# Second layer's cross-attention: four max products in every pair of tiles, and the mask of even tiles copied for two PSUM banks at once

## The chip, the cores and the metric

One core of a Trainium2 chip runs the kernel. The metric is the device time in microseconds; lower is better. Below, TensorE is PE in the profile (PEld its weight loads), VectorE is DVE, ScalarE is ACT.

## The reference, cut to what matters

Two layers follow each other, each a cross-attention to a context of 4096 rows and two smaller blocks. The change touches the second layer's attention alone (batch 2, 256 query rows, 16 heads of 16):

```python
Q = query @ Wq.T + bq; K = key @ Wk.T + bk; V = value @ Wv.T + bv
energy = jnp.einsum('bhqd,bhkd->bhqk', Q, K) / np.sqrt(HEAD_DIM)
energy = jnp.where(mask == 0, jnp.float32(-1e+20), energy)
attention = jax.nn.softmax(energy, axis=-1)
x = jnp.einsum('bhqk,bhkd->bhqd', attention, V)
return x.transpose(0, 2, 1, 3).reshape(b, -1, D_MODEL) @ Wo.T + bo
```

## The kernel before, in words

**The steps.** An attention is cut into 8 steps: four groups of four heads times two batches. A step k handles four heads of one batch against all 4096 keys. It needs the largest score of every query row first, so two things run beside each other: the softmax of step k, and the row maxima of step k+1.

**A step's softmax** goes over 32 tiles of 128 keys. For a tile, TensorE writes the scores of four heads (keys on the partitions, 4 x 256 query rows) into two PSUM banks: banks 0 and 1 for an even tile, 2 and 3 for an odd one (`at_pe_scores`, L533, four matmuls of 256 columns). The row maximum is taken off in the same matmul: it stands, negated and split in three bf16 parts, in three extra rows of Q. ScalarE takes the exponential of both banks at once (`at_act_step`, L666, 128x1024), and TensorE multiplies with the values (`at_pe_values`, L546). In the second layer the mask is added in PSUM: the bank is first filled with the mask and the scores are accumulated onto it. Of each tile, the first bank is filled by TensorE (L525, identity times mask, 512 columns) and the second by ScalarE (L670, a copy of 128x512), right after it has read that bank's previous tile. Tiles 0 and 1 of a step have both banks filled by TensorE.

**Row maxima.** A step needs 64 max products, called units: TensorE computes scores of 128 query rows against 512 keys (`at_pe_unit`, L501), and VectorE adds the mask and reduces to a maximum (`at_dve_unit`, L587). They use the three banks 4, 5, 7 in turn, so TensorE can be three units ahead of VectorE (semaphore `at_seen`). After the 64th, VectorE works out the maximum and its three parts (`at_dve_top`, L622 to L630); TensorE transposes them with eight small matmuls (`at_pe_rows`, L512) into one of the three banks, and ScalarE copies them into Q (`at_act_rows`, L640). The third unit after these matmuls waits for ScalarE's copies (`at_qrows`).

**The order of the work** is written out. A step has 16 pairs of tiles, j = 0 to 15. `at_pe_step` issues, for pair j: some units, the scores of tile 2j+2, some units, the scores of tile 2j+3, some units, the values of tiles 2j and 2j+1. `UNITS_AT[j]` says how many units stand at the three places; the same table serves both layers. Units of pairs 0 to 12 belong to step k+1, those of pairs 13 to 15 (`OWN` = 13) already to step k+2. The row matmuls stand at the start of pair 14 (`ROWS_AT`). Pair 15 issues the scores of tiles 0 and 1 of the next step. `at_dve_step` follows the same table, with the maxima at the start of pair 13. `LEAD` units of step 1 are computed before step 0 (7), the first `DONE` of them (2) before the row matmuls (`at_pe`, `at_dve`). ScalarE's order is: exponential of tile i, then the mask of tile i+2; its row copies stand before the exponential of tile 30, the copy of the previous step's output after that of tile 1. In the last step there are no units, and ScalarE has a few extra activations in its middle.

**Loads.** SyncE loads keys and values in quarters, each when the values of the step before it have used its place (`at_load`).

Of the kernel before, what the change touches and what calls it, by code (L numbers as in the profile page):

```python
# [22 lines left out]
HG = 4  # L23
# [28 lines left out]
def units_at(k, j, part):  # L52

    first = sum(map(sum, UNITS_AT[OWN if j >= OWN else 0:j])) + sum(UNITS_AT[j][:part])
    first, k = (first, k + 2) if j >= OWN else (first + LEAD, k + 1)
    return [(k, first + m) for m in range(UNITS_AT[j][part] if k < STEPS else 0)]


def rows_before(k):

    return min(UNITS * (k + 1) + DONE, UNITS * STEPS)


def bank_turn(n):

    return n + max(0, n - DONE) // UNITS

# [9 lines left out]
def build(nc, A, out):  # L77
    ctx = ExitStack()
    with ctx:
# [398 lines left out]
        def unit_bank(k, u):  # L478
            return UBANK[bank_turn(UNITS * k + u) % 3]

        def rows_bank(k):
            return UBANK[(rows_before(k) + k) % 3]
# [5 lines left out]
        def at_pe_unit(e, L, k, u, bank=None):  # L488
# [6 lines left out]
            since = (n - DONE) % UNITS if n >= UNITS + DONE else UNITS  # L495
# [5 lines left out]
            e.matmul(PS[:, unit_bank(k, u) if bank is None else bank, :], Qz[0:ROWS, o:o + 128],  # L501
                     Kz[b][0:ROWS, hh, c * CH:c * CH + CH], start=True, stop=True).then_inc(sem("at_unit"), 1)

        def at_pe_rows(e, L, k):

            e.wait_ge(sem("at_mparts"), at_count(L, k, 1, 1))
            e.wait_ge(sem("at_seen"), at_count(L, 0, UNITS, rows_before(k) + 1))
            for hh in range(HG):
                p0 = 96 - 32 * (hh // 2)
                for tt in range(2):  # L510
                    o = (hh % 2) * T + tt * 128
                    m = e.matmul(PS[p0:p0 + 3, rows_bank(k), o:o + 128], mparts[:, :, 2 * hh + tt], identb[:, :],  # L512
                                 start=True, stop=True)
            m.then_inc(sem("at_rows"), 1)

        def at_pe_scores(e, L, k, i):
# [34 lines left out]
        def at_pe_units(e, L, k, j, part):  # L551
            for kk, u in units_at(k, j, part):
                at_pe_unit(e, L, kk, u)
# [16 lines left out]
        def at_dve_unit(e, L, k, u, bank=None):  # L570
            g, b = divmod(k, 2)
            q, hh, tt, c = unit(u)
            ps = PS[:, unit_bank(k, u) if bank is None else bank, :]
# [28 lines left out]
        def at_dve_units(e, L, k, j, part):  # L602
            for kk, u in units_at(k, j, part):
# [29 lines left out]
        def at_act_rows(e, L, k):  # L633
            g, b = divmod(k, 2)
            e.wait_ge(sem("at_rows"), at_count(L, k, 1, 1))
            for m_ in range(2):
# [3 lines left out]
                e.activation(to[:, :, b * T:b * T + T], PS[p0:p0 + 3, rows_bank(k), :].rearrange("p (h t) -> p h t", h=2),  # L640
# [10 lines left out]
        def at_act_step(e, L, k):  # L651
            for i in range(NT):
# [15 lines left out]
                if L == 1 and i + 2 < NT:  # L668
# [1086 lines left out]
```

## Time and profile before

| | us |
|---|---|
| median of 3 runs | 1411.46 |
| lowest, highest | 1409.7, 1416.26 |
| the profiled execution's own time | 1413.51 |
| its span | 1411.7 |

Over the span: TensorE busy 89%, VectorE 73%, ScalarE 66%, GpSimd 14%. "Busy" sums whole stages, and a matmul's end is modelled, so TensorE's share says little about whether it waits. The second layer's attention runs from about 883 to 1316 us of the span; before it 64 units of step 0 run alone, from 840.

### The profile page before, as it was taken

How to read it: one execution, taken by the hardware profiler on the slowest of the kernel's cores; microseconds unless marked ns; L12 is line 12 of the kernel's file. 1: busy time of each engine (PE TensorE's matmuls, PEld its weight loads, DVE VectorE, ACT ScalarE, POOL GpSimd, SP SyncE). 2: the span in 40 equal slices, each digit the busy share in tenths (PEclk: the TensorE clock that was granted, in tenths of full speed). 3: DMA queues.
4: the chain of work that ended last, by engine and by line, in shares of the span. 5: the costliest groups of instructions: out<-in, count | busy, mean ns of one | idle time of the engine just before them, and what ended most of it. 6: DMA issues, size and time to landing. Idle time of an engine off the chain costs nothing.

```text
span 1411.7 us, 25663 instructions
## 1 busy us (share of the span) xinstructions
PE 1253.6 (89%) x8952; PEld 649.6 (46%) x8952; DVE 1024.8 (73%) x2276; ACT 927.0 (66%) x1203; POOL 203.0 (14%) x183
## 2 busy tenths in 40 slices
PE   7759999999999999789998539999999999998745
PEld 3436544444444445345555311445444444443523
DVE  3318799999999951479998449778778778763256
ACT  2317757667766775267664190999999999999304
POOL 2212200000000000069995040000000000000000
PEclk9979989999999999999999755999999999999976
DMA  4998785455545310127776874144343443300000
GB/s 150 216 250 275 246 206 115 96 124 114 129 93 114 62 63 31 37 84 244 250 259 196 205 115 104 36 88 81 73 92 69 85 84 70 62 22 2 1 0 15
DMA packets 100683, 160.97 MB, mean 114 GB/s; under 512 B 8496, under 2 KB 57136, under 8 KB 100064
## 3 DMA queue, kind: packets, MB, share of 16 engines
q1 hardware_dynamic: 99088, 158.13, 45.4%
q10 hardware_dynamic: 1488, 1.42, 0.4%
q8 instruction: 67, 1.10, 0.3%
q14 instruction: 40, 0.33, 0.1%
HBM read 114.34 MB, written 45.18 MB: 113 GB/s over the span
## 4 chain that ended last, share of the span: by engine, by line
PE 64%; DVE 13%; issue 12%; ACT 6%; POOL 2%; DMA 1%; DVEq 1%; SPq 1%; POOLq 0%; ACTq 0%
PE PS L546 17%; PE PS L501 16%; PE PS L533 15%; PE PS L525 4%; PE PS L274 3%; ACT Pz L666 2%; PE PS L283 2%; DVE Vz L1031 2%; DVE OT L1039 2%; DVE Kz L1031 1%; DMA Pz<-in_ctxT 1%; ACT Pz L664 1%; PE PS L791 1%; PE PS L821 1%; PE PS L785 1%
## 5 line engine op out<-in xcount | busy, mean ns | idle before, releaser
L666 ACT ACTIVATE Pz<-PS 128x1024 f32<-128x1024 f32 x488 | 483.2, 1018 | 110.9 <-PE PS L533 108.4
L587 DVE CUSTOM_DVE_ANT_0 Pz<-PS,Tz 128x512 bf16<-128x512 f32 x512 | 334.4, 689 | 88.0 <-PE PS L501 83.2
L501 PE MATMUL PS<-Kz,Qz 96*128 96x512 bf16 x1024 | 365.9, 401 | 31.6 <-issue 21.2
L533 PE MATMUL PS<-Qz,Kz 99*128 99x256 bf16 x2048 | 313.1, 274 | 5.1 <-ACT Pz L664 3.0
L584 DVE TENSOR_REDUCE mx<-PS 128x1 f32<-128x512 f32 x448 | 289.6, 687 | 13.8 <-PE PS L501 13.2
L546 PE MATMUL PS<-Pz,Vz 128*17 128x256 f32 x4096 | 271.4, 383 | 0.2
L533 PEld LDWEIGHTS PS<-Qz,Kz 99*128 99x128 bf16 x2048 | 192.9, 98 | 129.5 <-ACT Pz L664 10.4
L501 PEld LDWEIGHTS PS<-Kz,Qz 96*128 96x128 bf16 x1024 | 99.4, 98 | 196.8 <-DVE mx L587 78.6
L546 PEld LDWEIGHTS PS<-Pz,Vz 128*17 128x17 f32 x4096 | 94.1, 97 | 132.0 <-issue 63.4
L670 ACT ACTIVATE PS<-Tz 128x512 f32<-128x512 bf16 x240 | 144.3, 601 | 7.6
L525 PE MATMUL PS<-Tz,identb 128*128 128x512 bf16 x272 | 104.8, 385 | 8.7 <-ACT Pz L666 8.5
L352 POOL TENSOR_TENSOR Pz<-Pz 128x512 bf16<-128x512 f32 x64 | 79.1, 1246 | 145.4 <-ACT Pz L314 145.2
L392 POOL TENSOR_TENSOR rstd<-vare,nhalf 128x4 f32<-128x4 f32 x6 | 6.1, 1013 | 590.7 <-DVE vare L381 590.7
L274 PE MATMUL PS<-Pz,Vz 128*128 128x512 f32 x128 | 64.0, 624 | 21.6 <-DMA Pz<-in_ctxT 15.2
L331 DVE TENSOR_TENSOR Pz<-PS,Pz 128x512 f32<-128x512 f32 x32 | 21.9, 688 | 58.3 <-ACT Pz L299 58.3
L283 PE MATMUL PS<-Kz,Pz 128*128 128x256 f32 x256 | 62.0, 385 | 2.5 <-ACT Pz L309 1.4
L299 ACT ACTIVATE Pz<-PS 128x512 bf16<-128x512 f32 x32 | 19.1, 597 | 67.0 <-DMA k_parts<-Pz 34.2
L937 ACT ACTIVATE PS<-Kz,acoef 128x510 f32<-128x510 f32 x64 | 42.8, 686 | 29.7 <-DVE Kz L1031 16.3
L283 PE MATMUL PS<-Vz,Pz 128*128 128x256 f32 x256 | 61.5, 383 | 0.7 <-ACT Pz L309 0.6
L274 PE MATMUL PS<-Pz,Kz 128*128 128x512 f32 x128 | 61.9, 606 | 0.0
L283 PEld LDWEIGHTS PS<-Kz,Pz 128*128 128x128 f32 x256 | 47.5, 190 | 28.3 <-ACT Pz L309 14.9
L581 DVE CUSTOM_DVE_ANT_0 Tz<-PS,Tz 128x512 bf16<-128x512 f32 x64 | 43.9, 686 | 19.3 <-PE PS L501 18.3
(218 smaller groups left out, 1211.1 us busy)
## 6 DMA issues: line engine op xcount, KB each, us to landing
k_parts<-Pz SPq DMA_DIRECT2D x192, 128.0 KB
Kz<-k_parts SPq DMA_DIRECT2D x64, 384.0 KB, 4.8
v_ones<-Pz SPq DMA_DIRECT2D x32, 544.0 KB, 4.9
Vz<-v_ones SPq DMA_DIRECT2D x64, 272.0 KB, 6.0
Pz<-in_ctxT SPq DMA_DIRECT2D x32, 512.0 KB, 5.8
Kz<-k_parts SPq DMA_DIRECT2D x64, 256.0 KB, 5.5
Kz<-k_parts SPq DMA_DIRECT2D x64, 128.0 KB, 5.9
Kz<-in_mask_pieces SPq DMA_DIRECT2D x16, 512.0 KB, 5.8
```

The source lines that it names most:

```text
L274: m = e.matmul(PS[:, 4 + half, :], wk[L][:, k, half * 128:half * 128 + 128], ctxb(s)[:, k, :], start=(k == 0), stop=(k == KC - 1))
L283: m = e.matmul(PS[:, 6, st * D:st * D + D], ctxb(s)[:, k, t * 128:t * 128 + 128], wv[L][:, k, :], start=(k == 0), stop=(k == KC - 1))
L352: e.tensor_tensor(kb(s, half, 2), kres(half), kb(s, half, 1), ALU.subtract)\
L501: e.matmul(PS[:, unit_bank(k, u) if bank is None else bank, :], Qz[0:ROWS, o:o + 128], Kz[b][0:ROWS, hh, c * CH:c * CH + CH], start=True, ...
L525: e.matmul(PS[:, bank, :].rearrange("p (h t) -> p h t", h=2), identb[:, :], maskTs[:, i:i + 1, :].broadcast_to([128, 2, T]), start=True, s ...
L533: m = e.matmul(PS[:, bank, o:o + T], Kz[b][0:KROWS, hh, i * 128:i * 128 + 128], Qz[0:KROWS, q:q + T], start=(L == 0), stop=True, skip_grou ...
L546: m = e.matmul(PS[32 * hh:32 * hh + VW, 6, 0:T], Vz[:, b, o:o + VW], probs(i)[:, hh * T:hh * T + T], start=(i == 0), stop=(i == NT - 1), s ...
L581: e.tensor_tensor_reduce(bjunk[:, u % 3, :], ps, bias_rows[:, hh, o:o + CH][:, ::-1], 1.0, LOWEST, ALU.add, ALU.max, to).then_inc(sem("at_ ...
L584: e.tensor_reduce(to, ps, AX.X, ALU.max).then_inc(sem("at_seen"), 1)
L587: e.tensor_tensor_reduce(junk[:, u % 3, :], ps, masks[:, tt, c * CH:c * CH + CH], 1.0, LOWEST, ALU.add, ALU.max, to).then_inc(sem("at_seen ...
L666: m = e.activation(probs(i), PS[:, 2 * (i % 2):2 * (i % 2) + 2, :].rearrange("p a n -> p (a n)"), ACT.Exp)
L670: e.activation(PS[:, 2 * (i % 2) + 1, :].rearrange("p (h t) -> p h t", h=2), maskTs[:, i + 2:i + 3, :].broadcast_to([128, 2, T]), ACT.Iden ...
```

## The change

It gives each layer a table of its own. The first layer's is the old one. The second layer's has (1, 1, 2) for every pair: four units in each of 16 pairs. So `LEAD` for the second layer is 12 (7 before) and `DONE` 4 (2 before). And the masks of the second layer: for even tiles from tile 2 on, ScalarE copies the mask into both banks with one activation of 128x1024, and TensorE adds none; for odd tiles, TensorE fills both banks and ScalarE copies nothing. TensorE's even scores wait for that copy ahead of the first of the four instead of the third.

```diff
-UNITS_AT = ((1, 1, 1),) + ((1, 2, 2), (1, 1, 2)) * 6 + ((1, 0, 1), (1, 1, 2), (0, 0, 1))
+UNITS_AT = (((1, 1, 1),) + ((1, 2, 2), (1, 1, 2)) * 6 + ((1, 0, 1), (1, 1, 2), (0, 0, 1)),
+            ((1, 1, 2),) * 16)
 OWN = 13
 ROWS_AT = 14
-LEAD = sum(map(sum, UNITS_AT[OWN:]))
-DONE = sum(map(sum, UNITS_AT[OWN:ROWS_AT]))
+def total(L, j0, j1):
+
+    return sum(map(sum, UNITS_AT[L][j0:j1]))
+
+
+LEAD = [total(L, OWN, NT // 2) for L in range(2)]
+DONE = [total(L, OWN, ROWS_AT) for L in range(2)]
...
+def units_at(L, k, j, part):
+
+    first = total(L, OWN if j >= OWN else 0, j) + sum(UNITS_AT[L][j][:part])
+    first, k = (first, k + 2) if j >= OWN else (first + LEAD[L], k + 1)
+    return [(k, first + m) for m in range(UNITS_AT[L][j][part] if k < STEPS else 0)]
...
 in at_pe_scores:
-                if L == 1 and (hh == 0 or hh == 2 and i < 2):
+                if L == 1 and hh % 2 == 0 and (i % 2 or i < 2):
                     e.matmul(PS[:, bank, :].rearrange("p (h t) -> p h t", h=2), identb[:, :],
                              maskTs[:, i:i + 1, :].broadcast_to([128, 2, T]), start=True, stop=False,
                              skip_group_check=True)
-                elif L == 1 and hh == 2:
-
-
-                    e.wait_ge(sem("at_masked"), at_count(0, k, NT - 2, i - 1))
+                elif L == 1 and hh == 0:
+
+
+                    e.wait_ge(sem("at_masked"), at_count(0, k, NT // 2 - 1, i // 2))
...
 in at_act_step:
-                if L == 1 and i + 2 < NT:
+                if L == 1 and i + 2 < NT and i % 2 == 0:
                     e.wait_ge(sem("at_exp"), at_count(L, k, NT, i + 3))
-                    e.activation(PS[:, 2 * (i % 2) + 1, :].rearrange("p (h t) -> p h t", h=2),
-                                 maskTs[:, i + 2:i + 3, :].broadcast_to([128, 2, T]), ACT.Identity)\
+                    e.activation(PS[:, 0:2, :].rearrange("p a (h t) -> p (a h) t", h=2),
+                                 maskTs[:, i + 2:i + 3, :].broadcast_to([128, HG, T]), ACT.Identity)\
                         .then_inc(sem("at_masked"), 1)
...
 in at_pe (at_dve alike):
-            for u in range(DONE):
+            for u in range(DONE[L]):
                 at_pe_unit(e, L, 1, u)
             at_pe_rows(e, L, 0)
             e.wait_ge(sem("at_ones"), B * HG * (L + 1))
-            for u in range(DONE, DONE + 2):
+            for u in range(DONE[L], DONE[L] + 2):
                 at_pe_unit(e, L, 1, u)
             for i in range(2):
                 at_pe_scores(e, L, 0, i)
-            for u in range(DONE + 2, LEAD):
+            for u in range(DONE[L] + 2, LEAD[L]):
                 at_pe_unit(e, L, 1, u)
```

The other lines pass the layer L on to `units_at`, `rows_before`, `bank_turn`, `unit_bank` and `rows_bank`, which read `DONE[L]` and `LEAD[L]`.

## Rows read from the trace of the kernel before

**Rows 1.** The page's first part: busy time and share of each engine
```profile
PE 1253.6 (89%) x8952; PEld 649.6 (46%) x8952; DVE 1024.8 (73%) x2276; ACT 927.0 (66%) x1203; POOL 203.0 (14%) x183
```

**Rows 2.** Busy us by stage: stage, length, PE, PEld, DVE, ACT, POOL, PEclk, DMA share, GB/s
```profile
830.00:886.00 56.00, 43.76 (x86) 8.81 (x87) 42.72 (x141) 19.21 (x9) 12.43 (x7) 0.50 0.64 115
1153.50:1207.00 53.50, 52.90 (x488) 26.41 (x487) 42.94 (x132) 50.03 (x65) 0.00 (x0) 1.00 0.43 81
1260.50:1316.00 55.50, 46.46 (x446) 18.75 (x447) 16.42 (x35) 54.14 (x73) 0.00 (x0) 1.00 0.05 15
```

**Rows 3.** The chain of waits, two pairs of a step: start, us, what
```profile
1111.77 0.32 PE PS L501
1112.09 0.22 PE PS L525
1112.31 0.44 PE PS L533 x4
...
1113.62 0.43 PE PS L501 x2
1114.06 0.99 PE PS L546 x16
...
1118.57 0.32 PE PS L501
```

**Rows 4.** Who waited for whom, 890 to 1310 us: total, times, longest
```profile
ACT Pz L666 <- PE PS L533: 16.6, 44, 0.8
```

**Rows 5.** The timeline at a seam between steps: start, us, engine, instruction, idle before
```profile
1151.79 0.39 PE L512 MATMUL PS<-identb,mparts 128*3 128x128 bf16 x8
...
1152.11 0.39 PE L501 MATMUL PS<-Kz,Qz 96*128 96x512 bf16 x1
...
1152.75 0.60 ACT L670 ACTIVATE PS<-Tz 128x512 f32<-128x512 bf16 x1
...
1154.61 1.94 ACT L666 ACTIVATE Pz<-PS 128x1024 f32<-128x1024 f32 x2
...
1154.64 0.61 PE L501 MATMUL PS<-Kz,Qz 96*128 96x512 bf16 x2 [0.60 <-ACT Qz L640]
```

**Rows 6.** The chain in the last step, two exponentials one pair apart
```profile
1279.40 1.02 ACT Pz L666
...
1282.55 1.02 ACT Pz L666
```

**Rows 7.** Groups by line and form, 890 to 1310 us
```profile
L666 ACT ACTIVATE Pz<-PS 128x1024 f32<-128x1024 f32 x250 | 252.5, 1013 | 18.4 <-PE PS L533 16.6
...
L670 ACT ACTIVATE PS<-Tz 128x512 f32<-128x512 bf16 x235 | 141.3, 601 | 7.5
```

**Rows 8.** The timeline before step 0
```profile
880.35 0.22 DVE L622 TENSOR_REDUCE mneg<-mx 128x8 f32<-128x64 f32 x1
...
881.38 0.69 DVE L587 CUSTOM_DVE_ANT_0 Pz<-PS,Tz 128x512 bf16<-128x512 f32 x1
...
883.36 0.61 PE L525 MATMUL PS<-Tz,identb 128*128 128x512 bf16 x1
...
886.75 1.97 PE L501 MATMUL PS<-Kz,Qz 96*128 96x512 bf16 x4
...
887.57 0.69 DVE L587 CUSTOM_DVE_ANT_0 Pz<-PS,Tz 128x512 bf16<-128x512 f32 x1 [3.25 <-PE PS L501]
...
888.18 0.69 DVE L587 CUSTOM_DVE_ANT_0 Pz<-PS,Tz 128x512 bf16<-128x512 f32 x1
888.32 0.10 PEld L501 LDWEIGHTS PS<-Kz,Qz 96*128 96x128 bf16 x1 [1.00 <-DVE mx L587]
...
888.55 0.38 PE L525 MATMUL PS<-Tz,identb 128*128 128x512 bf16 x1
```

**Rows 9.** The chain of waits, row copies at two seams in turn
```profile
1099.27 0.59 ACT Qz L640
...
1153.38 0.59 ACT Qz L640
```

More of the change, by code:

```diff
@@ L44, with rows_before, bank_turn @@
 STEPS = 2 * NG
-UNITS_AT = ((1, 1, 1),) + ((1, 2, 2), (1, 1, 2)) * 6 + ((1, 0, 1), (1, 1, 2), (0, 0, 1))
+UNITS_AT = (((1, 1, 1),) + ((1, 2, 2), (1, 1, 2)) * 6 + ((1, 0, 1), (1, 1, 2), (0, 0, 1)),
+            ((1, 1, 2),) * 16)
 OWN = 13
 ROWS_AT = 14
-LEAD = sum(map(sum, UNITS_AT[OWN:]))
-DONE = sum(map(sum, UNITS_AT[OWN:ROWS_AT]))
[L52 to L66, printed above, removed]
+def total(L, j0, j1):
[6 more added lines that the diff above has]
+    return [(k, first + m) for m in range(UNITS_AT[L][j][part] if k < STEPS else 0)]
+def rows_before(L, k):
+    return min(UNITS * (k + 1) + DONE[L], UNITS * STEPS)
+def bank_turn(L, n):
+    return n + max(0, n - DONE[L]) // UNITS
 def unit(u):
@@ L476, in at_load, with unit_bank, rows_bank @@
                 at_load_values(e, L, g, b, q)
[L478 to L482, printed above, removed]
+        def unit_bank(L, k, u):
+            return UBANK[bank_turn(L, UNITS * k + u) % 3]
+        def rows_bank(L, k):
+            return UBANK[(rows_before(L, k) + k) % 3]
         def at_count(L, k, scale, more=0):
@@ L494, in at_pe_unit @@
             n = UNITS * k + u
-            since = (n - DONE) % UNITS if n >= UNITS + DONE else UNITS
+            since = (n - DONE[L]) % UNITS if n >= UNITS + DONE[L] else UNITS
             if since == 2:
@@ L500, in at_pe_unit @@
             o = (HG * g + hh) * R + b * T + tt * 128
-            e.matmul(PS[:, unit_bank(k, u) if bank is None else bank, :], Qz[0:ROWS, o:o + 128],
+            e.matmul(PS[:, unit_bank(L, k, u) if bank is None else bank, :], Qz[0:ROWS, o:o + 128],
                      Kz[b][0:ROWS, hh, c * CH:c * CH + CH], start=True, stop=True).then_inc(sem("at_unit"), 1)
@@ L506, in at_pe_rows @@
             e.wait_ge(sem("at_mparts"), at_count(L, k, 1, 1))
-            e.wait_ge(sem("at_seen"), at_count(L, 0, UNITS, rows_before(k) + 1))
+            e.wait_ge(sem("at_seen"), at_count(L, 0, UNITS, rows_before(L, k) + 1))
             for hh in range(HG):
@@ L511, in at_pe_rows @@
                     o = (hh % 2) * T + tt * 128
-                    m = e.matmul(PS[p0:p0 + 3, rows_bank(k), o:o + 128], mparts[:, :, 2 * hh + tt], identb[:, :],
+                    m = e.matmul(PS[p0:p0 + 3, rows_bank(L, k), o:o + 128], mparts[:, :, 2 * hh + tt], identb[:, :],
                                  start=True, stop=True)
@@ L551, in at_pe_units @@
         def at_pe_units(e, L, k, j, part):
-            for kk, u in units_at(k, j, part):
+            for kk, u in units_at(L, k, j, part):
                 at_pe_unit(e, L, kk, u)
@@ L572, in at_dve_unit @@
             q, hh, tt, c = unit(u)
-            ps = PS[:, unit_bank(k, u) if bank is None else bank, :]
+            ps = PS[:, unit_bank(L, k, u) if bank is None else bank, :]
             if L == 0 and b == 0 and u == 0:
@@ L602, in at_dve_units @@
         def at_dve_units(e, L, k, j, part):
-            for kk, u in units_at(k, j, part):
+            for kk, u in units_at(L, k, j, part):
                 at_dve_unit(e, L, kk, u)
@@ L639, in at_act_rows @@
                 to = Qz[96:99, o:o + 2 * R].rearrange("p (h r) -> p h r", h=2)
[L640 removed]
+                e.activation(to[:, :, b * T:b * T + T], PS[p0:p0 + 3, rows_bank(L, k), :].rearrange("p (h t) -> p h t", h=2),
                              ACT.Identity).then_inc(sem("at_qrows"), 1)
@@ L731, in at_dve @@
             at_dve_top(e, L, 0)
-            for u in range(DONE + 2):
+            for u in range(DONE[L] + 2):
                 at_dve_unit(e, L, 1, u)
@@ L736, in at_dve @@
                     at_dve_bias(e, 0, i)
-            for u in range(DONE + 2, LEAD):
+            for u in range(DONE[L] + 2, LEAD[L]):
                 at_dve_unit(e, L, 1, u)
```

## The prediction, made before the changed kernel was run

> **What bounds the kernel now.** I read the page first. TensorE is busy for 89% of the span [rows 1], which hides stages with different limits, so I cut the span by stage. The change lies in the second layer's attention, from 883 to 1316 us. There the steps last about 54 us each. In one of them TensorE shows 52.90 us of work in 53.50, ScalarE 50.03 and VectorE 42.94, with the clock granted in full; in the last step, which has no max products, TensorE drops to 46.46 in 55.5 and ScalarE rises to 54.14 [rows 2]. So two engines are close together, and the chain must decide which one sets the pace. It runs on TensorE alone through the pairs of tiles: a pair with four max products takes 3.28 us (1111.77 to the end of its values, 1114.06 + 0.99 = 1115.05), one with five takes 3.52 (to 1118.57) [rows 3]. ScalarE waits for TensorE's scores, 44 times and 16.6 us in all [rows 4], so it has slack in the middle of a step. It lacks slack at two places. At the seam between steps it is late with the rows of maxima, and TensorE stands still for 0.60 us in front of the third max product of pair 14 [rows 5]. In the last step it sets the pace: two tiles take 3.15 us [rows 6].
>
> **What the change removes and adds.** Over a full step TensorE does the same work: 64 max products, 34 mask matmuls (one more on each odd tile from tile 3, one fewer on each even tile from tile 2), 128 scores, 128 values. So no gain can come from TensorE's work, only from its waits. ScalarE has 30 mask copies of 0.601 us a step now [rows 7] and 15 of twice the size after. VectorE's reductions are the same in number, spread four to a pair. Layer 0 keeps its schedule. No DMA is moved on its queue; the keys of a pair are now read at most five products earlier, some 3 us, and a quarter of keys stays the unit of waiting, so loads cost nothing unless they were late, and no wait on them stands in the chain.
>
> **The price of the double copy.** No row shows a copy of 128x1024 from the mask. Lower end: 1.00, about the shortest exponential of that size; upper end: two of today's, 1.20. The nearest row is the exponential of the same size on the same engine, 1.013 on average and 1.02 in the pairs [rows 6, 7]; I take 1.02: engine and size are the same, only source and function differ, and a copy of half the size takes 0.601, so another 512 elements would have to cost as much as the first with their fixed part to reach 1.20. The Trainium skill (ScalarE: Activation LUTs, "What ACT_TABLE_LOAD costs") states 186 ns plus 0.833 ns an element, so by it the copy would take 1.04, and the 15 of the last step would give 0.3 us less. The trace does not quite agree: its row has 1.02.
>
> **Is the mask there in time?** Today an even tile starts with a mask matmul and two scores that need no copy. After the change all its four scores wait for a copy that itself follows the exponential. Walk a pair from its first max product, with the pieces of [rows 3]: product to 0.32, even scores to 0.76, product to 0.98, two masks and four scores to 1.86, two products to 2.30, values to 3.28. A matmul's record ends 0.17 after the next may start (0.39 against 0.22, [rows 5]), so the even exponential runs from 0.95 to 1.97, the copy from 1.99 to 3.01, the odd exponential from about 2.95 to 3.97. The next even scores want the copy at 3.28 + 0.32 = 3.60: 0.59 to spare. The next odd masks want the odd exponential at 3.28 + 0.98 = 4.26: 0.29 to spare. Queued behind the waiting scores are everything else on TensorE, products included; but nothing waits. The pace of a pair stays 3.28 and is TensorE's. What covers the copy is those 0.29 us; a copy of 1.20 still fits.
>
> **A full step.** Pairs 0 to 13 cost 14 x 3.28 = 45.9. In pair 13 the fourth product needs VectorE, which first works out the row maxima (1.03 us, 880.35 to 881.38 before step 0, [rows 8]); the walk brings both engines there at about 2.1 us, and I put 0.1 on it. Pair 14 adds the eight small row matmuls, 0.33 (1151.79 to 1152.11, [rows 5]), and its first product no longer follows values: 3.28 + 0.33 - 0.10 = 3.5. Its third product needs ScalarE's row copies. ScalarE no longer copies the mask of tile 31 (now 1152.75, right before them [rows 5]), so the copies, 1.2 long, run from 3.97 to 5.17 after the start of pair 13, while TensorE arrives at 5.5 because it has a mask more and the earlier pair is longer. The wait is gone with some 0.3 to spare. Pair 15 has four products where it had one, and four masks: 3.28 + 2 x 0.22 = 3.7. Sum 53.2, with rounding 53.3, against 54.11 now (1099.27 to 1153.38, [rows 9]): 0.8 less. Six such steps: **-4.8 us**.
>
> **The start.** VectorE's pace in front of step 0 is 0.61 us for a product (887.57 to 888.18), and TensorE may be three ahead. Twelve products stand before step 0 instead of seven. Four instead of two precede the row matmuls, and these now wait until the second is reduced: two reductions later, 1.3 us (today the maxima are ready at 881.38 and the scores run from 883.36). The six products after the first scores take VectorE's pace where three did not: product 6 starts at 886.75 + 1.3 = 888.05, its reduction is seen 1.57 later (as 886.75 to 888.32 now), and three more intervals of 0.61 bring the first product of step 0 to 891.45 and the scores to 891.7 against 888.55 [rows 8]. **+3.1 us**. Nothing hides this: ScalarE and TensorE both wait.
>
> **Step 6** has 52 products instead of 57. Its pairs 0 to 12 now take 3.06 + 6 x (3.52 + 3.28) = 43.9 (a pair of three products is one of 0.22 shorter than one of four) and then 13 x 3.28 = 42.6: -1.2. Its last three pairs have no products, and ScalarE saves one copy's fixed part there and starts a little earlier: -0.3. **Step 7** is ScalarE's. A pair is 3.15 now; after it two copies of 0.60 are one of 1.02, and the two exponentials that follow each other overlap (1.94 for two, [rows 5]), which together with one handover fewer is 0.22. TensorE follows: its masks, scores and values take 0.88 + 1.03 after an odd exponential. 15 x 0.22 = **-3.3 us**. What follows the attention is a serial chain and moves with it.
>
> Sum: 3.1 - 4.8 - 1.2 - 0.3 - 3.3 = **-6.5 us**. Against the profiled execution's own 1413.51 us (span 1411.7) that is 1407.0. That execution lies 2.05 above the median of the three runs; on the median, 1411.46, it gives **1405.0**.
>
> **The rivals.** A: the forecast, -6.5. The double copy at its ends, 1.00 and 1.20, shifts step 7 by -0.3 or +2.7, and small waits for a reduction in today's pairs of five may also go. B: the start costs nothing more, because the clock rises while the scores are still running and the products catch up: -9.6, 1401.9. For it: today's rise comes between 886.75 and 888.55, about where the scores would now be. Against it: the 0.61 is VectorE's, no clock helps it.
>
> C: the wait at the seam stays. ScalarE has only 0.3 us to spare there; if it enters pair 13 a step's 0.8 us later than in the walk, TensorE stands before the third product as now, and six steps give nothing: -1.7, 1409.8. With the copy at 1.20 as well, 1412.5. Against it: ScalarE has one copy fewer before its rows, and TensorE arrives later.
>
> F: the clock. Before step 0 TensorE is granted half (0.50, [rows 2]), the level of 1.2 GHz, and a mask matmul of 883.36 takes 0.61 against 0.38 at 888.55, at 2.4 GHz [rows 8]. It rises now after the first run of matmuls without a pause. Later, and with pauses of 0.4 us between six products at VectorE's pace, the rise may slip past the start of step 0. The scores of two tiles took 3.39 at the lower level (883.36 to 886.75) and take half at the higher; one such stretch more at the lower costs 1.6: -4.9, 1406.6. By the Trainium skill (TensorE: Matmul & The Clock Gate, "Why this matters for your kernels") TensorE has to be kept busy without gaps to reach the full clock, which speaks for F; the trace agrees so far as 64 products with pauses left it at 0.50.
>
> D: slower. The double copy is long, since it reads one mask row four times and writes two banks. Its place is between the even and the odd exponential, where a pair of ScalarE is the copy plus 1.92 us (an exponential with its handover, the other overlapped). It decides from 1.36 on, where that passes 3.28. At 1.50 each of 15 pairs in seven steps costs 0.14 (14.7 us) and each in step 7 costs 0.48 (7.2): -6.5 + 21.9 = +15.4, 1426.9. The result is slower by more than can be told from about 1.43. Against it: that is more than twice today's copy of half the size, which already broadcasts its row to two heads.
>
> **How the numbers follow.** A measurement of this kernel can tell some 0.5%, 7 us. Chances: A 0.52, B 0.17, C 0.12, F 0.13, D 0.06. The forecast sits just inside the band: of A, 0.20 falls beyond 7 us (a little more saved at each seam, or the error of a median of three runs that span 6.6 us), and of B 0.16. Faster 0.36; slower is D, 0.06; the rest 0.58. The range should hold 8 times in 10: it runs from B with a little more saved, 1401.5, to C with part of a longer copy, 1410.5; outside lie D and the tails of B and C.
>
> **What would show it.** In the profile after: copies of 128x1024 at 1.02, 120 of them; pairs of 3.28 throughout in the chain; no idle of TensorE before the third product of pair 14; row copies 53.3 apart; scores of tile 2 in step 0 about 3 us later after the last reduction; pairs of 2.93 in step 7. Wrong would be an even tile's scores waiting for the copy, ScalarE in the chain within steps 0 to 5, or a clock of 0.5 past step 0's first pairs.

## The result and the profile after

The changed kernel takes **1410.33 us**, the median of 20 executions (1407.95 to 1415.9), against 1414.78 for the kernel before (20 executions, 1409.7 to 1419.35) on the same chip. The ratio is 0.9974 with a 95% interval of 0.9963 to 0.9985: 3.7 us faster, 2.1 to 5.2. That is inside the half per cent that I had called no change, and 1410.33 lies just inside the range; on the 1411.46 shown ahead of the prediction the ratio gives 1407.8. The forecast was -6.5 us and 1405.0. The sign is right and the size is 57% of the forecast.

The profiled execution of the changed kernel has a time of its own of 1415.9 us (span 1413.8), 2.4 **longer** than that of before (1413.51, 1411.7). It is also the longest of that kernel's 20 executions, so one profile against one says little as a whole, and one has to cut it. I use three kinds of marks that both kernels have: the first reduction of the second layer's row maxima (the "top"), ScalarE's row copies near the end of each step, and the last copy of the attention's output. Up to the top no code differs, yet the changed kernel's execution is 3.46 later there (883.81 against 880.35 [rows 8]); the top lay anywhere from 878.57 to 884.34 in the profiles of this study. Behind the attention the profile is 1.30 longer. The attention itself is 2.67 shorter. So profiles are compared by the stretches of the attention, and whole times by ratios alone.

| stretch, us | before | after | measured | forecast |
|---|---|---|---|---|
| start: top to the row copies in step 0 | 56.24 | 60.35 | +4.11 | +2.3 |
| five: from there on, five steps | 270.90 | 266.62 | -4.28 | -4.0 |
| six: the interval after these | 53.98 | 53.10 | -0.88 | -1.5 |
| last: last row copies to the last output copy | 55.73 | 54.11 | -1.62 | -3.3 |
| sum | 436.85 | 434.18 | -2.67 | -6.5 |

The page of the changed kernel, first part:
```profile
PE 1258.1 (89%) x8951; PEld 655.7 (46%) x8952; DVE 1025.1 (73%) x2276; ACT 907.6 (64%) x1083; POOL 203.3 (14%) x183
```
Against [rows 1], ScalarE has 120 instructions fewer and 19.4 us less, VectorE the same, and TensorE 4.5 us **more**, though its list of work has the same length. A longer busy time at equal work is the first hint at a lower clock.

One step and the last one, in the columns of [rows 2], from the same points of the step:
```profile
1156.90:1210.20 53.30, 53.26 (x494) 26.87 (x490) 43.44 (x134) 48.26 (x51) 0.00 (x0) 1.00 0.42 81
1263.50:1319.00 55.50, 47.38 (x463) 21.61 (x462) 16.41 (x35) 51.61 (x58) 0.00 (x0) 0.97 0.05 16
```
In a full step TensorE is now busy for 53.26 of 53.30 us where 0.60 was free before, and ScalarE has 48.26 where it had 50.03. The last step reads 0.97 in the column of the clock; [rows 2] have 1.00 there.

The instructions of the new mask copy's line (minimum, median and maximum in ns), which answer to the copies of [rows 7]:
```profile
L678 ACT ACTIVATE PS<-Tz x120: 1027/1028/1030, 891.2 to 1313.0; 128x1024 f32<-128x1024 bf16 x120
```
The double copy takes 1.028, forecast 1.02. The Trainium skill (ScalarE: Activation LUTs, "What ACT_TABLE_LOAD costs") gives an estimate of 1.04 by its figures; the row lies between the two, and for 15 copies the one miss is +0.1 us and the other -0.2.

The chain of waits over a pair, as in [rows 3]:
```profile
1111.00 0.32 PE PS L509
1111.32 0.44 PE PS L541 x4
...
1113.29 0.99 PE PS L554 x16
1114.28 0.32 PE PS L509
```
From first product to first product it is 3.28, now in every pair up to pair 12, with TensorE alone on the chain.

The seam, as in [rows 5]:
```profile
1210.26 0.39 PE L520 MATMUL PS<-identb,mparts 128*3 128x128 bf16 x8
...
1210.59 0.39 PE L509 MATMUL PS<-Kz,Qz 96*128 96x512 bf16 x1
...
1210.78 1.20 ACT L648 ACTIVATE Qz<-PS 3x512 bf16<-3x512 f32 x2
...
1212.00 1.94 ACT L674 ACTIVATE Pz<-PS 128x1024 f32<-128x1024 f32 x2
...
1212.35 0.59 PE L509 MATMUL PS<-Kz,Qz 96*128 96x512 bf16 x2
```
The two products of 1212.35 that follow the row matmuls and the first odd scores have no idle time in front; the 0.60 of before is gone. ScalarE's row copies start at 1210.78 and 53.32 us earlier at 1157.46 (54.11 in [rows 9]). ScalarE has the slack now, as the view of who waited for whom shows from 890 to 1310 us, against 16.6 and 44 in [rows 4]:
```profile
ACT Pz L674 <- PE PS L541: 37.5, 100, 3.3
```

The start, as in [rows 8]:
```profile
883.81 0.22 DVE L630 TENSOR_REDUCE mneg<-mx 128x8 f32<-128x64 f32 x1
...
888.21 0.61 PE L533 MATMUL PS<-Tz,identb 128*128 128x512 bf16 x1 [0.17 <-ACT Qz L648]
...
891.59 4.02 PE L509 MATMUL PS<-Kz,Qz 96*128 96x512 bf16 x7
...
895.41 1.06 PE L541 MATMUL PS<-Qz,Kz 99*128 99x256 bf16 x4
...
899.38 1.06 PE L554 MATMUL PS<-Pz,Vz 128*17 128x256 f32 x8
```
First scores 4.40 after the top, product 6 7.78 after it, scores of tile 2 (895.41) 11.60. By the forecast's own steps these were 4.3, 7.7 and 11.35. But a mask matmul or a pair of scores still takes 0.63, and the first values (899.38) run 1.06 for eight where sixteen take 1.06 later. Busy times and clock around this place and around a place in the last step:
```profile
886.00:890.00 4.00, 3.73 (x18) 1.55 (x18) 2.68 (x10) 2.46 (x3) 0.00 (x0) 0.50 0.00 0
890.00:895.00 5.00, 4.90 (x13) 1.41 (x11) 2.58 (x9) 2.99 (x3) 0.00 (x0) 0.50 0.01 3
895.00:900.00 5.00, 5.00 (x23) 2.32 (x26) 3.27 (x11) 3.08 (x3) 0.00 (x0) 0.50 0.00 0
900.00:904.00 4.00, 4.00 (x45) 1.82 (x34) 2.63 (x9) 2.18 (x3) 0.00 (x0) 0.93 0.00 0
1294.00:1297.00 3.00, 0.90 (x4) 0.46 (x5) 1.73 (x4) 2.97 (x6) 0.00 (x0) 0.92 0.00 0
1297.00:1300.00 3.00, 3.00 (x23) 1.10 (x22) 2.90 (x4) 1.96 (x2) 0.00 (x0) 0.52 0.00 0
```
The clock granted is 0.50 (1.2 GHz) up to 900 and rises to 1.00 (2.4 GHz) in the stretch after it, nearly 17 us after the top; before, it rose 8 us after the top. And there is a second hole, 0.92 and 0.52 at 1294 to 1300, that the kernel before does not have. Its stretches at these places:
```profile
886.00:890.00 4.00, 3.91 (x19) 1.74 (x18) 2.43 (x7) 3.12 (x5) 0.00 (x0) 0.72 0.01 2
890.00:895.00 5.00, 5.00 (x52) 2.28 (x50) 4.21 (x15) 4.91 (x7) 0.00 (x0) 1.00 0.01 2
1294.00:1297.00 3.00, 1.85 (x21) 0.69 (x21) 2.67 (x5) 2.94 (x5) 0.00 (x0) 1.00 0.00 0
1297.00:1300.00 3.00, 2.60 (x30) 1.10 (x26) 2.83 (x6) 2.94 (x5) 0.00 (x0) 1.00 0.00 0
```
The timeline of the changed kernel at the second hole:
```profile
1287.13 1.92 ACT L674 ACTIVATE Pz<-PS 128x1024 f32<-128x1024 f32 x2
...
1290.05 1.92 ACT L674 ACTIVATE Pz<-PS 128x1024 f32<-128x1024 f32 x2
...
1292.97 2.17 ACT L1186 ACTIVATE Kz<-Kz 128x512 f32<-128x512 f32 x4
...
1296.10 0.39 PE L533 MATMUL PS<-Tz,identb 128*128 128x512 bf16 x1 [2.33 <-ACT Pz L674]
...
1297.58 1.91 PE L554 MATMUL PS<-Pz,Vz 128*17 128x256 f32 x16
...
1300.29 1.02 ACT L674 ACTIVATE Pz<-PS 128x1024 f32<-128x1024 f32 x1 [1.33 <-PE PS L541]
...
1301.06 1.06 PE L554 MATMUL PS<-Pz,Vz 128*17 128x256 f32 x16
```
ScalarE's pairs are 2.92 apart (1287.13 to 1290.05; forecast 2.93; 3.15 in [rows 6]). Then come its four decay activations (2.17 us, L1186), TensorE has nothing to do for 2.33, and right after that its clock falls (0.52 in the row from 1297): sixteen values take 1.91 instead of 1.06, the scores of the next tile are late, and ScalarE waits 1.33 for them. Both kernels have these activations at this place, and TensorE of the kernel before waits as long behind them, without a fall of its clock:
```profile
1295.13 0.39 PE L525 MATMUL PS<-Tz,identb 128*128 128x512 bf16 x1 [2.44 <-ACT Pz L666]
```

So two theories go into the experiments. **Clock**: all that the forecast misses is two stretches of TensorE at 1.2 GHz, one at the start and one after the decay activations; the schedule itself gives what was worked out. **Schedule**: part of it is that one of the two edits gives less than forecast (the table or the masks), or takes back what the other gives.

### The profile page after: what moved, and what is told of

Read it like the earlier page. It is cut to its first block, busy times and chain, and to the rows that moved or that the text cites. A ratio compares the mean times of both kernels' runs of the same rounds, so it can differ in the third digit from the quotient of the medians.

```text
span 1413.8 us, 25662 instructions
## 1 busy us (share of the span) xinstructions
PE 1258.1 (89%) x8951; PEld 655.7 (46%) x8952; DVE 1025.1 (73%) x2276; ACT 907.6 (64%) x1083; POOL 203.3 (14%) x183
## 4 chain that ended last, share of the span: by engine, by line
PE 67%; DVE 13%; issue 9%; ACT 5%; DMA 2%; SPq 2%; POOL 1%; DVEq 1%; POOLq 0%; ACTq 0%
PE PS L554 17%; PE PS L509 16%; PE PS L541 16%; PE PS L533 4%; PE PS L282 3%; PE PS L291 3%; DMA Pz<-in_ctxT 2%; DVE Vz L1039 2%; DVE OT L1047 1%; ACT Pz L674 1%; DVE Kz L1039 1%; ACT Pz L672 1%; PE PS L799 1%; PE PS L829 1%; PE PS L419 1%
## 5 line engine op out<-in xcount | busy, mean ns | idle before, releaser
L509 PE MATMUL PS<-Kz,Qz 96*128 96x512 bf16 x1024 | 371.1, 403 | 30.0 <-issue 22.5
L541 PE MATMUL PS<-Qz,Kz 99*128 99x256 bf16 x2048 | 331.9, 275 | 6.2 <-ACT Pz L672 3.0
L678 ACT ACTIVATE PS<-Tz 128x1024 f32<-128x1024 bf16 x120 | 123.4, 1028 | 3.8
L945 ACT ACTIVATE PS<-Kz,acoef 128x510 f32<-128x510 f32 x64 | 42.8, 687 | 30.1 <-DVE Kz L1039 16.6
L291 PEld LDWEIGHTS PS<-Vz,Pz 128*128 128x128 f32 x256 | 49.6, 194 | 18.8 <-issue 6.8
```

Of the source, the lines that this page charges most:

```text
L291: m = e.matmul(PS[:, 6, st * D:st * D + D], ctxb(s)[:, k, t * 128:t * 128 + 128], wv[L][:, k, :], start=(k == 0), stop=(k == KC - 1))
L509: e.matmul(PS[:, unit_bank(L, k, u) if bank is None else bank, :], Qz[0:ROWS, o:o + 128], Kz[b][0:ROWS, hh, c * CH:c * CH + CH], start=Tru ...
L541: m = e.matmul(PS[:, bank, o:o + T], Kz[b][0:KROWS, hh, i * 128:i * 128 + 128], Qz[0:KROWS, q:q + T], start=(L == 0), stop=True, skip_grou ...
L678: e.activation(PS[:, 0:2, :].rearrange("p a (h t) -> p (a h) t", h=2), maskTs[:, i + 2:i + 3, :].broadcast_to([128, HG, T]), ACT.Identity)\
L945: e.activation(v3(abar[m_])[:, :, 1:T], v3(dt)[:, :, 1:T], ACT.Exp, scale=acoef[:, bass.ds(n * DC + m_, 1)]).then_inc(sem("ssm_abar"), 1)
```

## The experiments

All kernels compute all that the reference asks for; those with filler matmuls write what nobody reads into a bank that is overwritten afterwards. Line numbers of helpers shift by what is inserted.

**1. The table alone.** The changed kernel with the masks of before.
```diff
-                if L == 1 and hh % 2 == 0 and (i % 2 or i < 2):
+                if L == 1 and (hh == 0 or hh == 2 and i < 2):
...
-                if L == 1 and i + 2 < NT and i % 2 == 0:
+                if L == 1 and i + 2 < NT:
```


> The changed kernel with the masks as before (ScalarE copies one bank of every tile, TensorE fills the other): the new table alone. I read four stretches of the second layer's attention, from the first reduction of the row maxima to the last output copy: start (to the second step's row copies), five steps, step 6, last step. Before: 56.2, 270.9, 54.0, 55.7 us; changed: 60.4, 266.6, 53.1, 54.1. Theory (the steps' gain comes from the table, since it moves TensorE's arrival past ScalarE's row copies, and ScalarE's pair of 3.15 still fits in 3.28): start 60.4, five steps 266.6 to 267.0, step 6 53.2, last step 55.7 as before; sum 0.5 to 1.5 us under the kernel before. Rival (the gain comes from ScalarE's lighter masks): five steps near 270, sum 2 to 4 us slower than before.

Measured: ratio 0.9982 (0.9970 to 0.9995). Start 58.13, where 60.4 was expected with the same products in front; five steps 267.12 (53.42 each), six 53.30, last 56.80. Against before the five steps give -3.78 of the whole change's -4.28, so the table carries most of what a step saves. The last stretch, which has no max product, is 1.08 longer than before, and its timeline says why:
```profile
1293.21 0.61 PE L533 MATMUL PS<-Tz,identb 128*128 128x512 bf16 x1 [2.44 <-ACT Pz L674]
1293.61 1.06 PE L541 MATMUL PS<-Qz,Kz 99*128 99x256 bf16 x4
1294.60 1.91 PE L554 MATMUL PS<-Pz,Vz 128*17 128x256 f32 x16
```
The gap is 2.44, as in the kernel before at the same place, but here TensorE's clock is down after it (0.61 for a mask matmul, 1.91 for sixteen values).

**2. The masks alone.** The kernel before with the new masks.
```diff
-                if L == 1 and (hh == 0 or hh == 2 and i < 2):
+                if L == 1 and hh % 2 == 0 and (i % 2 or i < 2):
...
-                if L == 1 and i + 2 < NT:
+                if L == 1 and i + 2 < NT and i % 2 == 0:
```


> The kernel before with the new masks alone and its old table. Theory: start as before, 56.2, because no product is moved in front of step 0 and the clock rises as it did; five steps 269.5 to 270.9, since ScalarE reaches the row copies only 0.2 us earlier; step 6 53.5 to 54.0; last step between 52.4 (pairs of 2.91 throughout) and 54.1 (if the clock falls at the decay factors as in the changed kernel). Sum 3 to 4.5 us under the kernel before, so as good as the whole change. Rival (masks carry the steps' gain): five steps at 267, sum 6 to 8 under.

Measured: ratio 0.9948 (0.9929 to 0.9967). Start 55.56, five 268.50, six 53.45, last 54.11, with the same hole of the clock in it. Five steps of 268.50 were below all that was expected: the masks alone give more than half of the step gain (-2.40 of -4.28). The timeline at the seam:
```profile
1148.96 1.20 ACT L640 ACTIVATE Qz<-PS 3x512 bf16<-3x512 f32 x2
...
1150.19 1.94 ACT L666 ACTIVATE Pz<-PS 128x1024 f32<-128x1024 f32 x2
...
1150.22 0.60 PE L501 MATMUL PS<-Kz,Qz 96*128 96x512 bf16 x2 [0.16 <-ACT Qz L640]
```
The wait in front of the third product is 0.16 where it was 0.60 [rows 5]: with one copy fewer, ScalarE comes to the rows earlier. Table and masks overlap there, as each alone takes most of the same wait away. The start is the old one, without five more products in front of it. The sum, 431.62, is 2.56 **shorter** than that of the whole change.

**3. The clock at the start.** The changed kernel with filler matmuls: 192 columns behind each of the last 32 products in front of step 0 that wait for VectorE, five of 512 before the fourth product of the next rows and three before the first scores.
```diff
                     at_pe_unit(e, L, 0, u)
+                    if u >= UNITS // 2:
+                        fill(e, 1, 192)
...
+                if L == 1 and u == DONE[L] - 1:
+                    fill(e, 5)
                 at_pe_unit(e, L, 1, u)
...
+            if L == 1:
+                fill(e, 3)
             for i in range(2):
                 at_pe_scores(e, L, 0, i)
```


> The changed kernel with extra mask matmuls into a free bank whose results are not used: 192 columns after each of the last 32 max products of step 0, five of 512 columns before the fourth product of step 1, three of 512 before the scores of tile 0. Nothing else moves. Theory (the start is dear because TensorE stays at 1.2 GHz until about 900 us, far into step 0): the clock is at 2.4 GHz before the scores of tile 0, these take 1.76 instead of 3.4 us, and the start comes down from 60.4 to 56.5 to 57.5; the rest as in the changed kernel; 3 to 4 us faster than that kernel. Rival (VectorE's pace before step 0 sets the start, the clock nothing): start 60 or more, time unchanged. If the fill does not raise the clock, the run tells nothing of either.

Measured: ratio 0.9945 (0.9927 to 0.9963). Start 55.93, five 266.63, six 53.10, last 52.64; the sum 428.31 is 5.87 below that of the changed kernel. Three of its stretches, the last one right behind the decay gap:
```profile
870.00:880.00 10.00, 7.66 (x34) 1.89 (x34) 10.00 (x35) 0.00 (x0) 0.00 (x0) 1.00 0.00 0
890.00:895.00 5.00, 4.33 (x33) 1.89 (x33) 5.00 (x17) 3.29 (x5) 0.00 (x0) 1.00 0.01 3
...
1290.00:1292.00 2.00, 1.77 (x22) 0.87 (x22) 1.87 (x4) 1.97 (x3) 0.00 (x0) 1.00 0.03 8
```
The clock is 1.00 from before the top on, and the start is 4.42 shorter. In this execution the clock also holds after the decay gap (1.00 at 1290), which no edit of this kernel touches; that gives the other 1.46, and shows that the fall does not follow from the code around the gap alone.

**4. Fewer products in front of step 0.** Six of the products that stand before step 0 go into the pairs 0 to 5 of step 0, one each, in part 2.
```diff
+    if L == 1 and k == 0 and j < OWN:
+        first += min(j, CATCH) - CATCH
+        n += part == 2 and j < CATCH
...
-            for u in range(DONE[L] + 2, LEAD[L]):
+            for u in range(DONE[L] + 2, LEAD[L] - (CATCH if L == 1 else 0)):
```


> The changed kernel, but the six max products between the first scores and step 0 are issued inside it, one more in each of pairs 0 to 5 (five products a pair there). Theory: they no longer run at VectorE's pace (0.61 us each) but cost TensorE 0.22 to 0.24 each, and TensorE has no pauses after the first scores, so its clock rises early, about 5 us after the scores begin; start 57 to 58.2 instead of 60.4, the rest as in the changed kernel; 2.2 to 3.4 us faster than it. Rival (the clock's rise is not tied to the pauses): start 59.3 to 60.

Measured: ratio 0.9941 (0.9924 to 0.9959). Start 56.35, five 266.62, six 53.11, last 52.65 (no fall). The start is 4.0 shorter, more than was expected. The six products in a row at VectorE's pace and the late clock are both gone here, since the clock rose 6 to 8 us after the top, as it does before; this run does not separate the two.

**5. The changed kernel again, the decay activations spread, and all together.** Three kernels measured together: the changed kernel as it is; the same with the four decay activations one each in front of tiles 16, 18, 20 and 22; and 3, 4 and 5 in one.
```diff
-                if i == NT // 2 and L == 1 and k == STEPS - 1:
-                    tm_act_decay(e)
+                if i in (16, 18, 20, 22) and L == 1 and k == STEPS - 1:
+                    tm_act_decay(e, (i - 16) // 2)
```


> The changed kernel once more, for a second profile of it. Theory (TensorE's clock rises before step 0, and falls at the decay factors of the last step, at a moment that is not tied to the kernel): five steps 266.6, step 6 53.1 again to 0.05, but the start anywhere from 57.5 to 60.4, and the last step either 52.7 (no fall) or about 54.1 (fall). Rival (both are fixed by the kernel's order of work): start 60.3 and last step 54.1 again, within 0.2.

> The changed kernel with ScalarE's four decay activations of the last step issued one each after tiles 16, 18, 20 and 22 instead of all four after tile 16, so that TensorE's gap of 2.3 us there becomes four short ones. Theory: the clock stays at 2.4 GHz through the last step, which takes 52.7 in the profile; over many runs 0 to 1 us faster than the changed kernel (it gains only in those runs whose clock falls). Rival: the long gap does not matter, the last step can show 54.1 with the factors spread too.

> The changed kernel with all three: the fill before step 0, the six products moved into step 0, the decay factors spread. Theory: start 54.0 to 55.0 (the fill gives the clock, 55.9 alone; the move saves VectorE's pace of three products more), five steps 266.6, step 6 53.1, last step 52.7; sum 426.5 to 427.5, that is 9 to 10 us under the kernel before, ratio 0.993 to 0.995. Rival (with the clock high the move saves nothing more): start 55.9, sum 428.3.

Measured: the changed kernel 0.9976 (0.9966 to 0.9986), spread decays 0.9972 (0.9962 to 0.9982), all 0.9937 (0.9924 to 0.9950). The changed kernel repeats its stretches: 60.38, 266.61, 53.11, 54.11. That is what the rival expected, by which the kernel's order of work fixes them; the next kernel and the third profile in experiment 7 (59.07 and 54.96) speak against it. With the decays spread, the last stretch is 52.64 and its timeline has gaps of 0.77 and no fall:
```profile
1295.22 0.39 PE L533 MATMUL PS<-Tz,identb 128*128 128x512 bf16 x1 [0.77 <-ACT Pz L674]
...
1296.20 1.06 PE L554 MATMUL PS<-Pz,Vz 128*17 128x256 f32 x16
...
1298.65 0.39 PE L533 MATMUL PS<-Tz,identb 128*128 128x512 bf16 x1 [0.77 <-ACT Pz L674]
```
Its start is the changed kernel's code, yet it took 57.09 instead of 60.35. The chain of waits shows the clock rise in the middle of the scores of tile 1, 7 us after the top:
```profile
891.05 0.43 PE PS L541 x2
891.47 0.22 PE PS L533
```
Two score matmuls of 256 columns, or one mask matmul of 512, take 0.43 up to there and 0.22 from there on. In the changed kernel's second profile the same chain still has 1.2 GHz at the first values, 15.65 after the top:
```profile
892.05 0.85 PE PS L541 x4
...
895.89 1.55 PE PS L554 x16
897.44 0.32 PE PS L509
```
Sixteen values take 1.55 there, partly at either level, and 0.99 in the steady pairs. So the two starts are alike in code and 3.3 us apart, and the clock is the only difference that the views show.

All three edits together have a sum of 427.98, but the move of the six products gives only 0.34 beyond the filler (start 55.59 against 55.93), as the rival expected. The timeline of it shows what is late next:
```profile
886.80 0.38 PE L516 MATMUL PS<-Kz,Qz 96*128 96x512 bf16 x1
888.35 0.60 PE L548 MATMUL PS<-Qz,Kz 99*128 99x256 bf16 x4 [1.17 <-ACT PS L685]
888.78 0.38 PE L516 MATMUL PS<-Kz,Qz 96*128 96x512 bf16 x1
```
TensorE waits 1.17 us for ScalarE's mask copy: without the products the even scores of tile 2 come before their double copy. This is the wait that the prediction looked for in the pairs. It also came with the moved products alone (0.68 us at that place); the changed kernel has it three times, 0.4 us at most, all in the last step.

**6. New masks on the old table, and a filler in the last step.** The masks alone with filler and spread decays; and kernel "all" with a filler of 384 columns behind each pair's values in the last step.
```diff
                 for part in range(2):
                     at_pe_values(e, L, k, 2 * j + part)
+                if L == 1 and k == STEPS - 1:
+                    fill(e, 1 if j < NT // 2 - 1 else 2, 384, 4)
```


> The kernel before with the new masks, the fill before step 0 (five of 512 columns before the row matmuls, three before the scores) and the spread decay factors, and the old table. Theory: start 53.3 to 54.3 (seven products in front instead of twelve, clock high), five steps 268.5 as with the masks alone, step 6 53.4, last step 52.8; sum 428 to 429, so 1 to 2 us behind the one with the new table and the six products moved. Rival (the new table's steps give nothing once the start is mended): sum at or under 427.

> The one with fill, six products moved and decay factors spread, and in the last step one more unused matmul of 384 columns into a free bank after the values of each pair, two after the last pair. Theory: TensorE has 0.2 to 0.3 us of idle per pair there, so the pace stays ScalarE's (last step 52.65 to 52.8) while the clock stays at 2.4 GHz up to the 32 small matmuls behind the attention, which take 3.75 us as in the best profiles instead of up to 5.25; 0 to 1.5 us faster than without. Rival: the fill delays the even tile's scores, last step 53.5 or more, no gain.

Measured: 0.9949 (0.9933 to 0.9965) for the first: start 54.14, five 268.50, six 53.45, last 52.65. Beside "all", which has the new table with six products moved, it shows the table at work with the clock out of the picture: the table costs 1.45 at the start and saves 1.88 over the five steps and 0.34 in the sixth interval, 0.8 in all. The timings (0.9949 and 0.9937) don't tell the two apart. The second has 0.9935 (0.9921 to 0.9948), the same as "all" within the intervals. Its chain of waits behind the attention:
```profile
1311.44 3.75 PE PS L808 x32
```
These 32 small matmuls take 3.75 as in the kernel before, 5.25 in the changed one, 5.19 in experiment 3 and 4.45 in "all"; but the last stretch is 0.5 longer (53.17). That the filler keeps the clock up there is not shown: the moved products alone, the spread decays alone and the two kernels of experiments 6 and 7 with the old table and filler have 3.75 without it.

**7. The filler on the kernel before, and two repetitions.** The first run asks how much of the gain is the filler's alone; three more filler matmuls stand before the first scores, as in experiment 3. The other two repeat the masks alone and the changed kernel.
```diff
                     at_pe_unit(e, L, 0, u)
+                    if u >= UNITS // 2:
+                        fill(e, 1, 192)
...
+            if L == 1:
+                fill(e, 5)
             at_pe_rows(e, L, 0)
```


> The kernel before with only the fill in front of step 0 (old masks, old table, decay factors together). Theory (the low clock at the start costs the kernel before as well, for the 3.4 us of the first scores): start 54.2 to 54.8 instead of 56.2, the other stretches as before; 1.4 to 2 us faster than before. Rival (the fill helps the changed kernel by something else): start 56.

> The new masks with the old table once more, to tell whether they alone are faster than the whole change. Theory: five steps 268.5 again (the even scores begin a mask matmul earlier, so ScalarE reaches the row copies earlier and TensorE's wait at the seam is 0.16 instead of 0.60), ratio to before 0.995 to 0.9975. Start 55.5 to 56.3, last step 52.7 or, with a fall of the clock, 54.1. Rival (the first timing was a stray): ratio 0.998 or above.

> The changed kernel a third time, beside the masks alone on the same chip. Theory: start anywhere from 57 to 60.4 (the clock's rise comes 6 to 17 us after the maxima), five steps 266.6, step 6 53.1, last step 52.7 or 54.1; ratio 0.997 to 0.998. Rival (start and last step are fixed by this kernel's order): 60.4 and 54.1 to 0.1.

Measured: filler on the kernel before 0.9987 (0.9975 to 0.9998), start 54.61 (1.63 shorter), five 270.89, last 56.38 with the clock's fall; masks alone 0.9972 (0.9960 to 0.9983), start 55.57, five 268.50, last 54.11; changed kernel 0.9970 (0.9955 to 0.9985), start 59.07, five 266.62, last 54.96. By the profiles, masks alone stay 2.1 to 2.6 shorter than the whole change, all of which had a late clock at the start; by the timings they were so once (0.9948) and were not the second time (0.9972). Which of the two kernels is faster is not settled.

**The clock in all profiles.** The clock granted in stretches of 2 us, counted from the top of each profile, and whether the clock fell in or right after the decay gap. The three kernels with filler and spread decays, left out here, have 1.00 in all these stretches and no fall:

| kernel | 4-6 | 6-8 | 8-10 | 10-12 | 12-14 | 14-16 | 16-18 | start | fell | last |
|---|---|---|---|---|---|---|---|---|---|---|
| before | .50 | .54 | 1.00 | 1.00 | 1.00 | 1.00 | 1.00 | 56.24 | no | 55.73 |
| masks alone | .50 | .67 | 1.00 | 1.00 | 1.00 | 1.00 | 1.00 | 55.56 | yes | 54.11 |
| masks alone again | .50 | .65 | 1.00 | 1.00 | 1.00 | 1.00 | 1.00 | 55.57 | yes | 54.11 |
| moved products | .50 | .71 | 1.00 | 1.00 | 1.00 | 1.00 | 1.00 | 56.35 | no | 52.65 |
| spread decays | .50 | .75 | 1.00 | 1.00 | 1.00 | 1.00 | 1.00 | 57.09 | no | 52.64 |
| table alone | .50 | .50 | .80 | 1.00 | 1.00 | 1.00 | 1.00 | 58.13 | yes | 56.80 |
| changed, third | .50 | .59 | 1.00 | .77 | .50 | .88 | 1.00 | 59.07 | yes | 54.96 |
| changed | .50 | .50 | .50 | .50 | .50 | .50 | .82 | 60.35 | yes | 54.11 |
| changed, again | .50 | .50 | .50 | .50 | .50 | .50 | .81 | 60.38 | yes | 54.11 |
| filler | 1.00 | 1.00 | 1.00 | 1.00 | 1.00 | 1.00 | 1.00 | 55.93 | no | 52.64 |
| filler on before | 1.00 | 1.00 | 1.00 | 1.00 | 1.00 | 1.00 | 1.00 | 54.61 | yes | 56.38 |

The three starts with the old table rise alike, 6 to 8 us after the top. So does the one with the six products moved. Of the five with the new table and all its products in front, only one does; one rises with them, falls back some 3 us later, about where the products run at VectorE's pace, and rises again; the others rise later. That it is the pauses between these products which put the rise off is argued and not shown: the spread decays have the same pauses and an early rise, and no run changed the pauses alone (experiment 4 takes the products away, experiment 3 fills other places too). With the gap of 2.3 to 2.4 us in the last step the clock fell in 7 profiles of 10; with gaps of 0.69 to 0.77 it fell in none of 4. No kernel profiled more than once showed both outcomes there (the changed one fell three times of three, masks alone twice of two), so whether the fall is a matter of the execution or of the kernel stays open. Its price differs too: with the new masks 1.5 us where the clock was down for one short stretch, and 2.3 in the changed kernel's third profile (54.96), where it stayed down longer.

The clock also varies where no profile was read. The mean granted clock of each of the changed kernel's 20 executions lies between 0.922 and 0.929, and the lower it is, the longer the execution: about 1 us for 0.001 (correlation -0.85). The profiled one has 0.923 and is the longest. That shows that part of the scatter goes with the clock, and not at which places it was low.

## Where the prediction was right, and the step that failed

**Full steps: right.** Pairs of 3.28, steps of 53.32 where 53.3 was written, no wait in front of pair 14's third product. In pair 13 the fourth product waits about 0.2 for VectorE, where 0.1 was put. Five steps give -4.28 for -4.0; most of the difference is that I took 54.11 for every step of before, and one of the five took 54.46. Rival C is out by the seam's timeline.

**The double copy: right.** 1.028 for 1.02. Rival D, decisive from 1.36 on, is out. The walk through a pair, which left 0.29 us of cover, held in the full steps: waits for the copy come to 1.1 us in all the attention, all of them in the last step.

**The last step, by its mechanism: right.** Pairs of 2.92 for 2.93. Without the clock's fall the stretch is 52.64 or 52.65 (experiments 3 and 4) against 55.73 without it before: -3.1 for -3.3. In the changed kernel it fell, for 1.46 more (54.11).

**The start: the delay right, the clock wrong.** The scores of tile 2 were to come 3.1 later after the top; they came 3.4 later (11.60 against 8.20), and 2.6 later with the spread decays (10.79). In the profile with a clock like that of before (spread decays), the stretch is 0.85 longer; in the changed kernel 4.11. The 3.26 between them are the clock at 1.2 GHz for nearly ten more us. That is rival F, which I had given 0.13. Its mechanism was named in full, down to the pauses between products at VectorE's pace; its size, 1.6, was taken from the scores of two tiles and is half of what it came to: masks, products, scores and values of the first pair went at 1.2 GHz as well (892.05 to 897.44 in the second profile's chain). Rival B, by which the start costs nothing more, is out: at a like clock it still costs 0.85, and 1.32 with filler in both kernels.

**The step that failed** is thus a term that the sum put at nothing: the clock. The forecast's start and last step both take the clock to rise and hold as in the kernel before; for the start F priced the other case, but the sum left it out, and for the last step it was not even written down. The runs show +3.3 us at the start and +1.5 in the last step in its place. With a like clock in both (spread decays for start, five and six; experiment 3 for the last stretch) the parts are +0.85, -4.29, -0.87 and -3.08, -7.4 in all, 0.9 **more** than forecast. The start gives 1.4 more than forecast and the five steps 0.3 more, the sixth interval 0.6 less and the last stretch 0.2 less. The start and the sixth interval are cut at the row copies, and I had put a whole step's 0.8 for the part ahead of the cut, while the pairs 14 and 15, which grow, lie behind it: the values of pair 0 come 12.86 after the top instead of 10.04 (+2.8 for the 3.1 of the forecast), those of pair 12 at 52.19 instead of 50.91, and the row copies at 57.09 instead of 56.24. Give back 3.3 at the start and 1.5 at the end, and the changed kernel's -2.67 is there. With filler in both kernels (experiments 3 and 7, the last stretch of before without its fall) the change is worth +1.32 - 4.26 - 0.87 - 3.08 = -6.9 by the profiles; by the timings (0.9945 against 0.9987) it is about -5.9, with wide intervals on both.

That the timings show -3.7 and the profiles -2.6 to -3.1 is no contradiction: the one profile of before had no fall in the last step. Two profiles of the old masks in which the clock fell have 56.80 and 56.38 for that stretch, 1.1 and 0.7 more. How often the late rise or the fall happens in executions that are not profiled is not shown by any run.

**What beats both.** All three additions (filler, six products moved, decays spread) give 0.9937, 1405.55 us against 1413.42, and with the filler in the last step 0.9935. Measured beside them, the changed kernel has 0.9976; the intervals don't touch. By the profiles the filler carries it (start 4.4) with the spread (last stretch 1.5), and the move gives almost nothing on top. The timings don't go so far: the filler alone (0.9945) and the move alone (0.9941) are as good as all three within the intervals, and the spread alone (0.9972) is not told apart from the changed kernel.

## What to carry to other kernels

When a change puts more waiting products, or any pauses, in front of a stretch in which TensorE is the bound, cost that stretch at both levels of the clock and give the lower one a real chance: here the delay was right to 0.3 us, and the clock raised the price of the start from 0.85 to 4.11. Try to fill or move the pauses of TensorE before shaving the work around them; here the filler gave the changed kernel about as much again as the change had given (0.9974 to 0.9945), and it gave the kernel before 0.9987. And where two profiles differ in a stretch whose code is equal, profile each kernel again before the difference is put down to the change.

## What the runs showed of the hardware that was not expected

In the changed kernel and the one with spread decays, whose code is equal up to there, the clock of 2.4 GHz comes 7, 8 or 17 us after the top, and once it came, went and came back within 7 us. The Trainium skill (TensorE: Matmul & The Clock Gate, "Why this matters for your kernels") wants TensorE busy without gaps. The filler runs agree in direction (1.00 throughout, in both kernels), though TensorE was not without gaps in them: it was busy for 7.66 of 10 us before the top. Gaps of 0.69 to 0.77 us in the last step held in four of four; with gaps of 2.3 to 2.4 us the clock fell in seven and held in three, with equal code around the gap.

The mask copy of 1024 elements took 1028 ns, of 512 elements 601: 427 ns for 512 elements, 0.834 ns each, which leaves 174 fixed (an estimate from these two sizes). In every profile the clock fell again soon after the attention, and the 32 small matmuls there took 3.75 us where it was granted in full up to their end, and 3.80 to 5.28 where it fell sooner.
